# Two attention layers on one core: the symmetric Gram matrix computed without its mirrored block, and ScalarE's group normalisations placed later in its queue

## The reference, cut to what matters

```python
# layer 0, per sample: x, y are [256, 2048]
q = Wq @ y + bq; k = Wk @ y + bk; v = Wv @ x + bv       # 8 heads of 32 channels
scores = einsum('hdl,hel->hde', q, k) / sqrt(256)        # = Wq (y y^T) Wk^T + bias terms
attn = softmax(scores)
o = Wo @ (attn v) + bo + x
x1 = groupnorm over the whole sample (o) * gn_w + gn_b
# layer 1, per sample: attention along positions in chunks of 64, q, k, v from y
u = (W_out @ chunk_attention(W_in y + b_in, mask) + b_out) * mask
out = instancenorm(u + x1)                               # per channel, over the 2048 positions
```

## Time and profile before

| | us |
|---|---|
| median of 3 runs (lowest, highest) | 1607.18 (1606.38, 1608.31) |
| the profiled execution | 1603.11 |
| its span, first to last instruction | 1601.0 |
| PE busy | 1553.0 (97%) |
| DVE busy | 1324.3 (83%) |
| ACT busy | 985.2 (62%) |
| POOL busy | 460.0 (29%) |
| Gram matmuls, L389, x512 | 133.8, 403 ns each |
| group normalisations, L581, x128 | 97.0, 813 ns each |

### The profile page before, as it was taken

The page is one execution under the profiler, slowest core; times in us unless marked ns, Lnnn a source line. Parts: engine busy times, 40 slices in busy tenths (PEclk is TensorE's granted clock), DMA queues, the critical chain, the costliest instruction groups (busy, mean ns, idle before and its releaser), DMA issues.

```text
span 1601.0 us, 53789 instructions
## 1 busy us (share of the span) xinstructions
PE 1553.0 (97%) x23816; PEld 1307.3 (82%) x23816; DVE 1324.3 (83%) x2008; ACT 985.2 (62%) x1780; POOL 460.0 (29%) x292
## 2 busy tenths in 40 slices
PE   7999999999999999999999999999999999999994
PEld 6888888888888888888888888888888888888873
DVE  4778879888798888979888788888978879888886
ACT  5556665656657666575565666566576665756743
POOL 1114233141331414224142331413314132141422
PEclk9999999999999999999999999999999999999998
DMA  6122331423323242241423314233142422414121
GB/s 239 58 98 75 107 110 48 143 81 114 106 76 119 68 140 81 92 128 42 147 84 97 115 53 146 76 119 107 55 137 70 131 90 81 125 57 140 41 67 66
DMA packets 96326, 157.20 MB, mean 98 GB/s; under 512 B 5344, under 2 KB 38240, under 8 KB 95968
## 3 DMA queue, kind: packets, MB, share of 16 engines
q1 hardware_dynamic: 96096, 153.78, 30.5%
HBM read 120.20 MB, written 33.55 MB: 96 GB/s over the span
## 4 chain that ended last, share of the span: by engine, by line
PE 88%; ACT 6%; DVE 4%; issue 1%; DMA 0%; POOL 0%; DVEq 0%; SPq 0%; POOLq 0%; ACTq 0%
PE pj_ps L281 42%; PE l_ps L281 11%; PE s_ps L305 7%; PE w_ps L316 6%; PE l_ps L389 6%; PE w_ps L334 6%; DVE yt_hl L698 3%; PE s_ps L294 2%; ACT o_sb L581 2%; PE l_ps L405 2%; PE l_ps L425 2%; ACT prob_t L568 1%; ACT yt_hl L540 1%; ACT prob L573 1%; PE l_ps L413 1%
## 5 line engine op out<-in xcount | busy, mean ns | idle before, releaser
L933 POOL TENSOR_TENSOR prob<-prob,row_inv 128x1024 f32<-128x1024 f32 x128 | 262.3, 2049 | 958.9 <-DVE row_inv L729 958.9
L591 ACT CAST att_hi<-w_ps 128x256 fp32r<-128x256 f32 x256 | 82.9, 378 | 252.7 <-PE w_ps L334 247.0
L281 PE MATMUL pj_ps<-y_hi,w_hi 128*128 128x512 f32 x512 | 208.5, 407 | 9.3 <-DVE y_lo L694 9.3
L281 PE MATMUL pj_ps<-y_hi,w_lo 128*128 128x512 f32 x512 | 202.2, 395 | 0.0
L281 PE MATMUL pj_ps<-y_lo,w_hi 128*128 128x512 f32 x512 | 202.2, 395 | 0.0
L724 DVE TENSOR_REDUCE row_sum<-prob 128x16 f32<-128x1024 f32 x128 | 154.9, 1210 | 47.5 <-ACT prob L573 47.5
L698 DVE TENSOR_TENSOR yt_hl<-yt_raw,yt_hl 128x1024 fp32r<-128x1024 f32 x64 | 117.4, 1834 | 83.4 <-ACT yt_hl L540 83.4
L712 DVE TENSOR_REDUCE row_max<-s_ps 128x16 f32<-128x1024 f32 x128 | 155.7, 1216 | 22.2 <-PE s_ps L305 21.1
L950 POOL TENSOR_TENSOR o_sb<-o_sb,u_sb 128x1024 f32<-128x1024 f32 x63 | 164.4, 2631 | 2.8 <-ACT o_sb L581 2.8
L568 ACT COPY prob_t<-w_ps 128x512 f32<-128x512 f32 x256 | 149.6, 585 | 21.6 <-PE w_ps L316 17.5
L719 DVE TENSOR_TENSOR prob<-s_ps,row_max 128x1024 f32<-128x1024 f32 x128 | 155.4, 1214 | 0.1
(11 more groups left out here) (107 smaller groups left out, 3519.8 us busy)
## 6 DMA issues: line engine op xcount, KB each, us to landing
y_raw<-in_ctx SPq DMA_DIRECT2D x64, 512.0 KB, 4.9
yt_raw<-in_ctx_t SPq DMA_DIRECT2D x64, 512.0 KB, 4.8
x_raw<-in_x SPq DMA_DIRECT2D x64, 512.0 KB, 5.0
out_z<-o_sb SPq DMA_DIRECT2D x64, 512.0 KB, 3.6
mask_b<-in_mask SPq DMA_DIRECT2D x64, 256.0 KB, 4.0
u_sb<-in_w SPq DMA_DIRECT2D x2, 512.0 KB, 5.0
w_sb<-in_w SPq DMA_DIRECT2D x1, 1024.0 KB, 10.9
cst<-in_consts SPq DMA_DIRECT2D x1, 512.0 KB, 7.0
```

The costliest lines, as they stand in the source:

```text
L281: last = mm(dst, lhs, rhs, start=i == 0, stop=i == len(todo) - 1)
L933: nc.gpsimd.tensor_tensor(cut, cut, row_inv[:, u % 2, :].unsqueeze(2).to_broadcast([P, 2 * HEADS, CHUNK]), ALU.mult).then_inc(probs_done, 1)
```

## The change

TensorE's second row half of the Gram product leaves out its first 128 columns (the block HH(1,0), the mirror image of HH(0,1)): 384 columns in place of 512. HL is still computed whole. VectorE adds only the blocks (0,0), (0,1) and (1,1); TensorE transposes three blocks of HL in slot 5 (`UPPER`), and VectorE's sum now releases `upper_done`. In slot 6 TensorE transposes the finished block G(0,1), and in slot 7 ScalarE copies it to G(1,0) (`copy_lower`) and releases `gram_done`, which T1 waits for. The four normalisations stand at the end of slots 2 and 3 (q = 0, 1) and early in slots 4 and 6 (q = 2, 3).

```diff
--- before.py
+++ after.py
@@ -33,6 +33,7 @@
 UT = BT // 2
 LAG = 2
 EPS = 1e-5
+UPPER = ((0, 0), (0, 1), (1, 1))
 W_HALF = 2 * HALVES * E
 NEG = -1e9
 SCALE0 = 1.0 / E ** 0.5
@@ -46,7 +47,7 @@
 
 S_SPLIT_T, S_GRAM, S_HL, S_HLT, S_SUM, S_T1, S_SC, S_U, S_M, S_X, S_MX = 0, 1, 4, 5, 6, 7, 8, 10, 11, 11, 12
 
-T_X1, T_Z, T_Z_STATS, T_STAT, T_FINAL, T_STORE = 1, 3, 4, 8, 10, 10
+T_Z, T_Z_STATS, T_STAT, T_FINAL, T_STORE = 3, 4, 8, 10, 10
 
 
 def build(nc, x, ctx, ctx_t, mask, w0, w1, cols, bk0, consts, out):
@@ -163,6 +164,7 @@
         av_ready, att_hi_done, att_lo_done = sem("av_ready"), sem("att_hi_done"), sem("att_lo_done")
         qkv_ready, qkv_copied = sem("qkv_ready"), sem("qkv_copied")
         wout_ready, u_done = sem("wout_ready"), sem("u_done")
+        upper_done, lower_ready = sem("upper_done"), sem("lower_ready")
         gram_ready, hl_copied, gram_half = sem("gram_ready"), sem("hl_copied"), sem("gram_half")
         hlt_ready, gram_done = sem("hlt_ready"), sem("gram_done")
         y_sum_step, y_sum_done = sem("y_sum_step"), sem("y_sum_done")
@@ -385,18 +387,21 @@
                     else:
                         pe.wait_ge(c1_done, 1)
                 for lb in range(PAIRS):
+                    hi_lo = yt_hl[:, lb, :, :].rearrange("p a c -> p (a c)")
                     for i in range(HALVES):
-                        last = mm(l0_ps[i][:, :].rearrange("p (a c) -> p a c", a=2), yt_hl[:, lb, 0, i * P:(i + 1) * P], yt_hl[:, lb, :, :],
+                        last = mm(l0_ps[i][:, i * P:], yt_hl[:, lb, 0, i * P:(i + 1) * P], hi_lo[:, i * P:],
                                   start=q == 0 and lb == 0, stop=q == BLOCKS - 1 and lb == PAIRS - 1)
                 last.then_inc(gram_ready, 1)
 
             def layer0(n, s):
                 if s == S_HLT:
                     pe.wait_ge(gram_half, count(n, 1, 0))
-                    for i in range(HALVES):
-                        for k in range(HALVES):
-                            last = nc.tensor.transpose(l0_ps[0][:, i * E + k * P:i * E + (k + 1) * P], hl[:, k, i * P:(i + 1) * P], ident)
+                    for i, k in UPPER:
+                        last = nc.tensor.transpose(l0_ps[0][:, i * E + k * P:i * E + (k + 1) * P], hl[:, k, i * P:(i + 1) * P], ident)
                     last.then_inc(hlt_ready, 1)
+                elif s == S_SUM:
+                    pe.wait_ge(upper_done, count(n, 1, 0))
+                    nc.tensor.transpose(l0_ps[0][:, E:E + P], gram[:, 0, P:E], ident).then_inc(lower_ready, 1)
                 elif s == S_T1:
                     pe.wait_ge(gram_done, count(n, 1, 0))
                     pe.wait_ge(y_sum_done, count(n, 1, 0))
@@ -612,6 +617,10 @@
                     last = copy(hl[:, i, :], l0_ps[i][:, E:2 * E])
                 last.then_inc(hl_copied, 1)
 
+            def copy_lower(n):
+                act.wait_ge(lower_ready, count(n, 1, 0))
+                copy(gram[:, 1, 0:P], l0_ps[0][:, E:E + P]).then_inc(gram_done, 1)
+
             def copy_u0(n):
                 act.wait_ge(u0_ready, count(n, 1, 0))
                 copy(u0[:, :, :], l0_ps[1][:, :].rearrange("p (i o) -> p i o", i=HALVES)).then_inc(u0_copied, 1)
@@ -641,16 +650,18 @@
                     u, e = divmod(s, 2)
                     if e == 0 and not (first and u < LAG):
                         copy_att(n, u - LAG)
+                    if not first and s in (4, 6):
+                        group_normed(n - 1, s // 2)
                     if e == 1 and not (first and u == 0):
                         copy_pt(n, u - 1, 1)
                     if s == S_HL:
                         copy_hl(n)
+                    if s == S_SUM + 1:
+                        copy_lower(n)
                     if s == S_SC + 1:
                         layer0_exponents(n)
                     if S_MX <= s < S_MX + BLOCKS:
                         copy_output(n, s - S_MX)
-                    if e == 1 and not first and T_X1 <= s < T_X1 + BLOCKS:
-                        group_normed(n - 1, s - T_X1)
                     if S_X <= s < S_X + BLOCKS:
                         split_x(n, s - S_X)
                     if S_SPLIT_T < s < S_SPLIT_T + BLOCKS:
@@ -669,8 +680,8 @@
                         split_y(n, b + 2)
                     if s == S_U:
                         copy_u0(n)
-                    if e == 0 and not first and T_X1 <= s < T_X1 + BLOCKS:
-                        group_normed(n - 1, s - T_X1)
+                    if not first and s in (2, 3):
+                        group_normed(n - 1, s - 2)
                     if s == SLOTS - 1 and not last:
                         split_yt(n + 1, 0)
 
@@ -745,11 +756,13 @@
                 if s == S_HL:
                     dve.wait_ge(hl_copied, count(n, 1, 0))
                     for i in range(HALVES):
-                        last = tt(gram[:, i, :], l0_ps[i][:, 0:E], hl[:, i, :], ALU.add)
+                        last = tt(gram[:, i, i * P:], l0_ps[i][:, i * P:E], hl[:, i, i * P:], ALU.add)
                     last.then_inc(gram_half, 1)
                 elif s == S_HLT:
                     dve.wait_ge(hlt_ready, count(n, 1, 0))
-                    tt(gram[:, :, :], l0_ps[0][:, :].rearrange("p (i c) -> p i c", i=HALVES), gram[:, :, :], ALU.add).then_inc(gram_done, 1)
+                    for i in range(HALVES):
+                        last = tt(gram[:, i, i * P:], l0_ps[0][:, i * E + i * P:(i + 1) * E], gram[:, i, i * P:], ALU.add)
+                    last.then_inc(upper_done, 1)
                 elif s == S_T1:
                     dve.wait_ge(t1_ready, count(n, 1, 0))
                     for i in range(HALVES):
```

## The result

The changed kernel takes 1581.44 us (median of 4 runs, 1577.74 to 1581.61) against 1606.78 us (4 runs, 1603.40 to 1608.31): a ratio of 0.9841, 95% interval 0.9829 to 0.9854, so 1.6% less, clear of what the measurement can't tell. The forecast was 1581, within 1577 to 1592.

What follows compares the result with a forecast made beforehand. TensorE, busy for 97% of the span, was taken to bound the kernel. From the median 1607.2 us, 14.4 for narrower Gram matmuls and 11.7 for the slot 4 stall came off: 1581 us, range 1577 to 1592.

Steps and rivals of the forecast that it cites:

- The bound: Whole kernel: TensorE, busy for 97% of the span, sets the pace, so work taken off it shortens the kernel.
- Term 1: Gram matmuls on TensorE: 256 of 512 narrowed from 512 to 384 columns, 56 ns each, saving 14.4 us.
- rival A: Narrower Gram matmuls save less: 1591 us by the skill's slope, 1584 by the weight load's limit; chance 0.06.
- The Trainium skill's spacing: Gram matmuls: about 131 ns at 512 columns, 81 at 128, so 128 columns save an estimated 17 ns, 4.3 us altogether.
- Term 2: Slot 4: TensorE's stall for VectorE's subtraction goes once slot 3's normalisation follows the split; 15 x 0.78 = 11.7 us saved.
- The subtraction's turn: Slot 3: VectorE's subtraction runs after GpSimd's scaling, from 525.1 to about 526.3 us, ahead of the join; 1.6 us spare.
- What was costed at nothing: Moved transpose, ScalarE's new copy, moved normalisations, later join and narrower addition: all expected off the path, 0 us.
- 0.2 us of room: Slot 7: ScalarE's new copy releases `gram_done` near 545.0 us, TensorE wants it at 545.20.
- The later join: Slot 6: GpSimd's fourth join, 542.0 to 544.4 us, holds VectorE's widening of y sums until 544.55, before TensorE's 545.20.
- Rival C: Slot 3: subtraction issued after the join starts, so the stall stays and only 14.4 us are saved, 1592.8 us; chance 0.05.
- the subtraction's longest: VectorE's subtraction of y transposed: its maximum time was to fall from 3.24 us to near 2.2.
- the 4.1 us: Whole kernel: the median of runs, 1607.2 us, lies 4.1 above the profiled execution, 1603.1; carried over to the forecast.

Runs made afterwards that it cites:

- experiment 1: The kernel before with only the four normalisations moved, the Gram product left whole: 1594.43 us, ratio 0.9921.
- Experiment 4: The changed kernel with the second row half of the Gram product at 512 columns again, all else kept: 1593.6 us, ratio 0.9916.
- experiment 6: The changed kernel with eight more unused 128-column copies on ScalarE ahead of the mirrored block's copy in slot 7: 1594.4 us, ratio 0.9929.
- experiment 8: The changed kernel with normalisations 0 to 2 back in their old slots, the fourth kept in slot 6: 1593.26 us, ratio 0.9916.
- one swap: The kernel before with only quarter 2's normalisation put behind the split of y transposed in slot 3: 1594.04 us, ratio 0.9922.
- two copies: The changed kernel with two more unused 128-column copies on ScalarE ahead of the mirrored block's copy in slot 7: 1580.23 us, ratio 0.9842.

## Why the prediction was right

**The bound.** TensorE sets the pace: right. What was taken off or put on it, or made it wait (experiments 1, 4, 6, 8), came out in the distance of samples.

**Term 1**, 14.4 us at 56 ns: right. Experiment 4 gives 57 ns by the distance of samples; its median time, 12.2 us, is too coarse to tell 56 from 44. The weight load is hidden behind 384 columns (rival A and its 44 ns fall). The Trainium skill's spacing (TensorE: Matmul & The Clock Gate, section Back-to-back issue gap) would have given an estimated 17 ns; no run here shows it, and the measured 57 decides.

**Term 2**, the stall of 0.78 us: right in size and cause; one swap gives 0.77. The subtraction's turn came as drawn, with the join put back.

**What was costed at nothing** cost nothing on the whole: experiments 1 and 4 have the same distance. I gave `gram_done` 0.2 us of room, it has 0.47 (two copies cost 0.05 us a sample at most, eight 1.01). The later join holds the y sums as foreseen, 2.02 us for the widening.

**What the sum lacked.** The moves gain 0.06 us a sample more on the old Gram product. On the narrow one the fourth move alone gains 0.22: 0.17 by the copy of the probabilities in slot 5, 0.06 by the attention copy in slot 6. I had looked at the third and fourth normalisations only for what their new places cost, not for what their old ones did.

**Where the reasoning failed though the number held.** Rival C was priced as term 1 alone, 14.4 us. The terms don't add: without the moves the narrow product gains 0.54 us a sample, about 9 us, since TensorE only comes sooner to a subtraction that doesn't (0.22) and to the copy in slot 5 (0.17). My forecast of the subtraction's longest was off too: near 2.2 us, measured 2.94 (the mean of all went from 1.83 to 1.87). In slot 1, where the split no longer stands behind a normalisation, it is now issued just behind the start of GpSimd's scaling:

```profile
505.38 2.93 DVE L709 TENSOR_TENSOR yt_hl<-yt_raw,yt_hl 128x1024 fp32r<-128x1024 f32 x1
...
505.33 1.90 POOL L946 TENSOR_TENSOR prob<-prob,row_inv 128x1024 f32<-128x1024 f32 x1 [1.77 <-DVE row_inv L740]
```

GpSimd's scaling began 0.05 us earlier and held it from 505.38 to 507.2. It ends at 508.31, the matmuls that need it start at 508.99, so it costs nothing. Before it was held in slot 1 too, but took 1.75 us.

**The sum against the medians.** 26.1 us forecast, 25.3 measured. Steady samples gave 1.75 us where the two terms make 1.68 (0.90 and 0.78; the prediction's 1.6 is the sum spread over 16 samples), about 1 us more in all. In the profiled pair odd gaps (1.1 us) and the start (1.2) take it back; which of these make up the medians' 0.8 us too little is not shown, and it lies within their interval. Against its own profiled execution the forecast was 4.6 us too low (1577.0 for 1581.6), 3.4 of it at the end, where I had taken the end as unchanged; the medians hide that, because most executions of the kernel before lose it too. That these lose it in the same stretch is concluded from their mean clocks and from the nine profiles without filling that do; they have no profile. By the same mean clocks the 4.1 us that I added between profile and median were mostly this clock, which I hadn't looked at: that they carried over to the changed kernel was luck.

## What to carry to other kernels

Where one engine sets the pace, look at each of its waits for the other engine's queue: what stands in that queue ahead of the work that is waited for, and could stand behind it? One swap was worth almost half of this change. Two savings on one path are not independent: what makes the waiting engine faster lengthens the wait, so remove the wait first, and read the rows of weight loads as well as those of matmuls. What such a row prints is idle time, part of which can be there without the wait: the loss is the difference to the same place in a run that doesn't wait.

## What I had not expected of the hardware

- At the very end, after gaps of TensorE of 0.58 and 1.30 us, its clock was at half in both profiles of the changed kernel, and still full after the same gaps in that of the kernel before: 3 to 4 us of 1580. With the gaps filled by idle matmuls it stayed at 1.00 up to the last projection in both profiles, and all nine executions were among the shortest.
- Some instructions of VectorE and GpSimd hold each other out whole. A copy of one 256-column input that takes 0.29 us alone took 2.02 us, all the rest waiting; 0.05 us decided in slot 1 who went first. Not all do so: beside the joins of slot 3 VectorE's `branch`, which reads the bank `pj_ps`, took its usual 0.74 us and `row_max`, which reads the scores, its 1.23, and two statistics instructions at 529.31 us took 1.22 beside GpSimd's scaling, 1.27 elsewhere.
